# A four-layer gated model on one core: layer 2's folded-values product in three float32r passes, with its operands split on ScalarE, GpSimd and VectorE

## The chip, the core and the metric

One core of a Trainium2 chip runs the whole program in one launch. The metric is the device time of that launch in microseconds (us), lower is better; times of the kernel before are the median of three runs. All rows below come from one profiled execution. In them PE is TensorE (matmul), PEld its weight load, DVE VectorE, ACT ScalarE, POOL GpSimd, SP the engine that issues most DMAs.

## The reference, cut to what matters

Four layers of gated cross-attention and feed-forward on `x` (2 x 1024 rows of 256), with a context of 77 rows. The change lies in layer 2's attention and at the end of the feed-forward network (FFN) before it.

```python
x = x + tanh(g_xattn[0]) * attention0(layernorm(x), ctx)
x = x + tanh(g_ffn[0]) * fp4_ffn(layernorm(x))
x = x + tanh(g_xattn[1]) * attention1(layernorm(x), ctx)
x = x + tanh(g_ffn[1]) * (relu(layernorm(x) @ W1 + b1) @ W2 + b2)      # layer 1's FFN
# layer 2's attention: 16 heads of width 64, 77 keys
xn = layernorm2(layernorm(x)); q = xn @ w_q; k, v = split(ctx @ w_kv)
scores = einsum('bqhd,bkhd->bhqk', q / 8, k)
attn = softmax(scores, axis=-1)
out = einsum('bhqk,bkhd->bqhd', attn, v).reshape(B, SQ, 1024) @ w_out + b_out
x = x + tanh(g_xattn[2]) * out * tanh(gate)
x = x + tanh(g_ffn[2]) * (layernorm(x) @ w_int4 + bias + layernorm(x) @ a @ b)
x = x + ...layer 3's attention, then its mixture of experts
```

## The kernel before, in words

The 2048 rows of `x` lie in SBUF as 16 tiles of 128 rows. The program is a series of stages, one function for each engine and stage (`ffn1_tensor`, `ffn1_vector`, `att2_tensor`, ...). Inside a stage the engines run their own instruction lists, which are written out by hand, and meet on semaphores; at the end of a stage every engine drains and waits for the other four (`end_stage`, one semaphore `stage_done`).

Layer 1's FFN goes through four groups of four tiles. A group has eight units `m` of 128 hidden columns: PE multiplies up (L1987) and, two units later, down (L2003), both as three passes of rounded float32r parts (high x high, high x low, low x high); ACT does the relu (L2054) and rounds it to its high part (L2059); DVE makes the low part (L2107). In the last group the other work of DVE is the quantisation of layer 2's FFN kernel (units 3 to 5), the statistics of tiles 0 and 1 for layer 2 (`lead_vector`, unit 6), and after the last unit the normalised tile 0 (`ln_apply_one`, L318 and L320), which PE waits for before it turns it (L2036) and goes on with the last down product. POOL meanwhile makes the low part of the folded key matrix `A2` (L870) and at the end the two reciprocal roots (`lead_pool`, L305).

Layer 2's attention works with matrices folded in advance: `A2` is the query projection times the keys, so that a tile's scores for all 16 x 77 = 1232 pairs of head and key are one product (L1498, in three banks of 462, 462 and 308 columns, three float32r passes); `VO` is the values times the output projection, so that the output is the 1232 probabilities (ten blocks of 128 pairs) times `VO` (L1520, in plain float32, ten products of 128 x 128 by 256 columns for each tile). In step `t` of the stage:

- PE: scores of tile t in parts j = 0, 1, 2, and behind each part the transposes of tile t-1's probabilities for the same j (L1508; chunks of 3, 4 and 3 blocks, into banks 3, 4, 3); layer 2's small FFN product of tile t-3 (L1529, L1537); the transposes of normalised tile t+1 (L1564); the output product of tile t-1 (L1520) and its bias (L1522).
- ACT: for each j the copy of the transposed probabilities of tile t-1 to SBUF (L1585), then the exponentials of tile t, one instruction of 77 columns for each head (L1593), with the negative maximum as bias; between them the copy L1604 and the rounding of tile t+1 to its high part (L1479).
- DVE: the two additions to `x` (L1648, L1652), the maximum of each score part (L1629), statistics (L295 to L300), the normalised tile t+2 (L318, L320), the low part of tile t+1 (L1485), and for each j the softmax's sum over 77 keys (L1638), its reciprocal (L1639) and the multiplication of the probabilities (L1640).
- POOL: the reciprocal roots (L305).

The waits that matter below: PE turns probabilities j after `norm_done` of DVE; bank 3 (j = 2) is filled again only after the copy of chunk 0 (`pt_copied`); the output product of chunk j waits for `pt_copied` of that chunk; the scores of tile t+1 wait for `x_lo`, which DVE's L1485 of step t gives. Probabilities and their transposes have two buffers each.

The output product before:

```python
for j, (c0, c1) in enumerate(PT2_CHUNKS):
    pe.wait_ge(s["pt_copied"], 3 * t + j + 1)
    for k in range(c0, c1):
        pe.matmul(bank[6][:, 0:D], probT2[p][:, k, :], vo[:, bass.ds(v0 + k * D, D)],
                  start=k == 0, stop=False, skip_group_check=True)
```

Steps 0 to 3 and the last ones are written out; the steps between run in a hardware loop of two steps (`pipeline`).

## Time and profile before

| | us |
|---|---|
| median of three runs | 1105.09 (1104.5 to 1105.19) |
| the profiled execution, its own time | 1102.33 |
| its span | 1100.5 |
| PE busy / PEld busy | 1045.6 (95%) / 898.1 (82%) |
| DVE busy | 779.4 (71%) |
| ACT busy | 536.3 (49%) |
| POOL busy | 172.1 (16%) |
| share of PE in the chain that ended last | 87% |

The span is the time from the first to the last instruction of the profiled execution; 1.8 us of its own time lie around it, and it is 2.8 us below the median. "Busy" counts an engine's own instructions; a share over the whole program mixes stages. The chain is followed back from the last instruction, at each step to what released it. In the timelines a row is a start, a duration and the operation, and instructions of one engine may overlap: the next one starts some hundredths before the one ahead of it has ended. A bracket is idle time before the row and what ended it.

### The profile page before, as it was taken

The page shows a single profiled execution, that of the slowest core. Times are in us where ns is not written, and L with a number is a line of the kernel's source. Part 1 is how long each engine was busy: PE and PEld are TensorE (multiplying, and loading weights), DVE is VectorE, ACT ScalarE, POOL GpSimd, SP SyncE. Part 2 cuts the span into 40 slices and gives each one's busy share as a digit, 9 for nine tenths or more (in the row PEclk, how much of TensorE's full clock was granted, in tenths as well). Part 3 has the DMA queues.
Part 4 walks back from the last instruction along what each step waited for, and adds up shares of the span by engine and source line. Part 5 has one row for each costly group of instructions (what it writes and reads, how often), then busy time and mean ns, then how long its engine had stood idle before and what let it go on. Part 6 is the DMA issues. An engine that isn't in the chain of part 4 may idle for free.

```text
span 1100.5 us, 18719 instructions
## 1 busy us (share of the span) xinstructions
PE 1045.6 (95%) x6208; PEld 898.1 (82%) x6208; DVE 779.4 (71%) x1779; ACT 536.3 (49%) x1279; POOL 172.1 (16%) x255
## 2 busy tenths in 40 slices
PE   4987899999999999999999998999999999999998
PEld 4865567777999979888888887999778888888887
DVE  5786779998887855458888867878674575555544
ACT  4677655533555565545554544566543333334222
POOL 2232001101112142230111100132330010000000
PEclk9798899999999999999999999999999999999999
DMA  9401010002000000000000005000021121122120
GB/s 287 108 1 42 1 12 1 0 1 77 2 1 0 1 12 2 1 1 1 1 0 0 1 1 244 1 0 1 1 80 66 57 80 49 60 78 64 51 84 30
DMA packets 30377, 41.22 MB, mean 37 GB/s; under 512 B 13615, under 2 KB 19577, under 8 KB 29414
## 3 DMA queue, kind: packets, MB, share of 16 engines
q1 hardware_dynamic: 29437, 39.63, 11.5%
q10 hardware_dynamic: 873, 0.72, 0.3%
q8 instruction: 39, 0.64, 0.2%
q14 instruction: 28, 0.23, 0.1%
HBM read 37.80 MB, written 2.54 MB: 37 GB/s over the span
## 4 chain that ended last, share of the span: by engine, by line
PE 87%; DVE 4%; ACT 4%; issue 1%; SPq 1%; DMA 1%; POOL 0%; DVEq 0%; PEldq 0%; ACTq 0%; POOLq 0%; PEld 0%
PE psum L2197 17%; PE psum L2208 9%; PE psum L1734 7%; PE psum L380 6%; PE psum L1520 6%; PE psum L1297 6%; PE psum L1268 5%; PE psum L1498 5%; PE psum L1987 4%; PE psum L2003 4%; PE psum L1742 4%; PE psum L1279 3%; PE psum L1208 2%; PE psum L1508 2%; PE psum L1537 1%
## 5 line engine op out<-in xcount | busy, mean ns | idle before, releaser
L305 POOL TENSOR_TENSOR rstd<-ve,mhalf 128x1 f32<-128x1 f32 x114 | 75.7, 665 | 561.0 <-DVE ve L300 560.8
L391 ACT COPY work<-psum 128x256 f32<-128x256 f32 (+2 forms) x241 | 99.2, 438 | 117.9 <-PE psum L380 111.2
L380 PE MATMUL psum<-ident,work 128*128 128x128 f32 (+2 forms) x596 | 95.2, 282 | 9.8 <-ACT zone L605 3.5
L2279 ACT CAST h_hi<-work 128x512 fp32r<-128x512 f32 x68 | 42.2, 621 | 122.8 <-DVE work L2350 95.5
L2340 DVE TENSOR_TENSOR work<-psum,work 128x512 f32<-128x512 f32 x68 | 46.9, 689 | 75.0 <-ACT work L2271 74.9
L380 PEld LDWEIGHTS psum<-ident,work 128*128 128x128 f32 (+2 forms) x596 | 73.3, 147 | 22.2 <-DVE xT_lo L1228 3.8
L2197 PE MATMUL psum<-x_hi,ew_hi 128*128 128x512 f32 (+1 forms) x272 | 87.2, 401 | 0.2
L2197 PE MATMUL psum<-x_lo,ew_hi 128*128 128x512 f32 (+1 forms) x272 | 85.3, 395 | 0.0
L2197 PE MATMUL psum<-x_hi,ew_lo 128*128 128x512 f32 (+1 forms) x272 | 84.8, 393 | 0.0
L1734 PE MATMUL psum<-early,work 128*128 128x352 f32 x256 | 82.4, 477 | 1.4 <-ACT zone L605 0.9
L2208 PE MATMUL psum<-ew_hi,h_hi 128*128 128x256 f32 x272 | 76.9, 283 | 2.4 <-DVE h_lo L2357 2.4
L2208 PE MATMUL psum<-ew_hi,h_lo 128*128 128x256 f32 x272 | 77.3, 284 | 0.0
L2208 PE MATMUL psum<-ew_lo,h_hi 128*128 128x256 f32 x272 | 76.8, 282 | 0.0
L2357 DVE TENSOR_TENSOR h_lo<-work,h_hi 128x512 fp32r<-128x512 f32 x68 | 46.9, 690 | 42.1 <-ACT h_hi L2279 42.0
L1297 PEld LDWEIGHTS psum<-zone,work 128*128 128x128 f32 x640 | 74.0, 192 | 0.2
L1297 PE MATMUL psum<-zone,work 128*128 (+2 forms) x640 | 74.2, 272 | 0.0
L2271 ACT ACTIVATE work<-psum 128x512 f32<-128x512 f32 x68 | 40.6, 596 | 69.0 <-PE psum L2197 68.8
L1734 PEld LDWEIGHTS psum<-early,work 128*128 128x128 f32 x256 | 49.4, 198 | 27.9 <-issue 3.0
L1520 PE MATMUL psum<-zone,work 128*128 128x256 f32 (+1 forms) x320 | 71.7, 379 | 0.0
L1520 PEld LDWEIGHTS psum<-zone,work 128*128 128x128 f32 x320 | 59.5, 190 | 7.7
L1593 ACT ACTIVATE work<-psum,small 128x77 f32<-128x77 f32 x256 | 62.5, 379 | 5.9 <-DVE small L1629 5.9
L1585 ACT COPY work<-psum 128x384 f32<-128x384 f32 (+1 forms) x48 | 27.0, 564 | 73.0 <-PE psum L1508 73.0
(285 smaller groups left out, 2596.9 us busy)
## 6 DMA issues: line engine op xcount, KB each, us to landing
work<-expert_shares SPq DMA_DIRECT2D x64, 256.0 KB, 3.2
early<-in_experts_in SPq DMA_DIRECT2D x1, 6528.0 KB, 18.5
x<-in_x_in SPq DMA_DIRECT2D x4, 512.0 KB, 6.7
early<-in_W_in SPq DMA_DIRECT2D x2, 1024.0 KB, 7.1
out_x<-x SPq DMA_DIRECT2D x3, 512.0 KB, 4.3
early<-in_Wk SPq DMA_DIRECT2D x1, 1024.0 KB, 6.1
early<-in_Wq SPq DMA_DIRECT2D x1, 1024.0 KB, 8.7
zone<-in_Wv SPq DMA_DIRECT2D x1, 1024.0 KB, 13.1
```

The costliest lines, as they stand in the source:

```text
L305: pool.tensor_tensor(rstd[:, slot:slot + 1], ve[:, slot:slot + 1], mhalf[:, 0:1], ALU.pow).then_inc(s["rstd_ready"], 1)
L380: last = pe.transpose(dst[0:rows, at:at + n], src, ident[0:n, 0:n])
L391: act.copy(dst, src).then_inc(s["tr_copied"], 1)
L1268: last = pe.matmul(bank[j][:, (a - h0) * SK:(z - h0) * SK], q_[:, k, :], key[:, bass.ds(col + (a - h0) * SK, (z - a) * SK)], start=(k, a, ...
L1297: last = pe.matmul(dst, probT[:, k, :], Vb[l][:, bass.ds(v0 + (k * 3 + a - a0) * vw, (z - a + 1) * vw)], start=k == mine[0], stop=k == min ...
L1498: last = pe.matmul(bank[j][:, 0:n], x_[:, k, :], a[k][0][:, bass.ds(col + a[k][1], n)], start=i == 0 and k == 0, stop=i == 2 and k == KD - 1)
L1520: pe.matmul(bank[6][:, 0:D], probT2[p][:, k, :], vo[:, bass.ds(v0 + k * D, D)], start=k == 0, stop=False, skip_group_check=True)
L1593: last = act.activation(prob[p][:, h * SK:(h + 1) * SK], bank[j][:, (h - h0) * SK:(h - h0 + 1) * SK], ACT.Exp, bias=nmx[:, h:h + 1])
L1734: last = pe.matmul(bank[c][:, 0:HALF], xnT[1 - p][:, k, :], wguT[:, k, c * HALF:(c + 1) * HALF], start=k == 0, stop=k == 1)
L2197: last = pe.matmul(bank[2 * which + e % 2][:], weights(w, e, which, k), a[:, k, cols], start=n == 0, stop=n == len(passes) - 1)
L2208: last = pe.matmul(bank[6 + j // 2][:, (j % 2) * D:(j % 2 + 1) * D], h[slot(e)][:, j * P:(j + 1) * P], weights(w, e, 2), start=e == 0 and ...
L2340: dve.tensor_tensor(esg[e % 2] if e < NE else hf[0], bank[2 + e % 2][:], esg[e % 2], ALU.mult).then_inc(s["u_read"], 1)
```

## The change

1. The output product runs in three float32r passes for each of the ten blocks. ACT rounds the transposed probabilities to `pT_hi` (two buffers, `pt_hi_done`), DVE subtracts from the same bank to get `pT_lo` (one buffer), and `pt_copied` is now given by DVE (`low_probabilities`), one subtraction behind each maximum.
2. `VO` is rounded in ten pieces of 128 x 512: ACT makes `vo_hi` (four pieces at the end of layer 1's FFN, one in step 0, three in step 1, two in step 2), POOL makes `vo_lo` in steps 0 to 2 (five, three, two pieces), ahead of its roots of that step. PE waits for five low pieces before tile 0's output product and for ten before tile 2's.
3. The sum over the keys is taken from DVE: the exponentials give it as their accumulator output (`accum_out`).
4. In the last group of layer 1's FFN the statistics of tiles 0 and 1 move from unit 6 to unit 1, the two roots on POOL behind piece 11 of `A2`, and the normalised tiles 0 and 1 into units 6 and 7; step -1 of layer 2 no longer makes tile 1.
5. A semaphore that nothing waited for (`vb_ready`) goes, and `shift` moves by two columns.

```diff
@@ -205,6 +205,10 @@
+        VO_WORDS = B * KT * D
+        vo_raw = VO.rearrange("p a b -> p (a b)")
+        vo_hi = rounded("vo_hi", early_at, KD * B * HK, [P, VO_WORDS])
+        vo_lo = rounded("vo_lo", zone2_at, KD * B * HK + 8 * D, [P, VO_WORDS])
...
@@ -403,7 +403,9 @@ (buffers of the transposed probabilities)
-        probT2 = [probT, carve(work, [at[0] + 2 * D], (KT, P))]
+        pT_hi = [rounded(f"pT_hi{k}", work_at, word, [P, KT, P]) for k, word in
+                 enumerate((common + 2 * KT * P, at[0] + 2 * D))]
+        pT_lo = rounded("pT_lo", work_at, common + 3 * KT * P, [P, KT, P])
...
+        def vo_pieces(t):
+            return range(0) if not isinstance(t, int) else {0: range(5), 1: range(5, 8), 2: range(8, 10)}.get(t, range(0))
...
@@ att2_tensor, outputs
+                if isinstance(t, int) and t in (0, 2):
+                    pe.wait_ge(w_lo_done, LO_BEFORE["VO"] + VO_PIECES * (1 if t == 0 else 2))
...
-                        pe.matmul(bank[6][:, 0:D], probT2[p][:, k, :], vo[:, bass.ds(v0 + k * D, D)],
-                                  start=k == 0, stop=False, skip_group_check=True)
+                        for i, (pr, vo) in enumerate(three((pT_hi[p], pT_lo), (vo_hi, vo_lo))):
+                            pe.matmul(bank[6][:, 0:D], pr[:, k, :], vo[:, bass.ds(v0 + k * D, D)],
+                                      start=k == 0 and i == 0, stop=False, skip_group_check=True)
...
@@ att2_scalar
-                act.copy(probT2[p][:, c0:c1, :], bank[PT2_BANKS[j]][:, 0:(c1 - c0) * P].rearrange("p (a b) -> p a b", a=c1 - c0)
-                         ).then_inc(s["pt_copied"], 1)
+                act.copy(pT_hi[p][:, c0:c1, :], bank[PT2_BANKS[j]][:, 0:(c1 - c0) * P].rearrange("p (a b) -> p a b", a=c1 - c0)
+                         ).then_inc(s["pt_hi_done"], 1)
...
-                                          ACT.Exp, bias=nmx[:, h:h + 1])
+                                          ACT.Exp, bias=nmx[:, h:h + 1], accum_out=rs[:, h:h + 1])
...
             def step(t, p):
+                for n in vo_pieces(t)[VO_EARLY if isinstance(t, int) and t == 0 else 0:]:
+                    act.copy(vo_piece(vo_hi, n), vo_piece(vo_raw, n)).then_inc(w_hi_done, 1)
...
@@ att2_vector
-                link(dve, dve.tensor_reduce(rs[:, h0:h1], pr, AX_X, ALU.add))
...
+            def low_probabilities(t, p, j):
+
+                c0, c1 = PT2_CHUNKS[j]
+                src = bank[PT2_BANKS[j]][:, 0:(c1 - c0) * P].rearrange("p (a b) -> p a b", a=c1 - c0)
+                dve.wait_ge(s["pt_hi_done"], 3 * t + j + 1)
+                if j == 0:
+                    wait(dve, s["y_ready"], t)
+                dve.tensor_tensor(pT_lo[:, c0:c1, :], src, pT_hi[p][:, c0:c1, :].bitcast(F32),
+                                  ALU.subtract).then_inc(s["pt_copied"], 1)
...
                 if has(t):
                     maximum(t, 0)
+                if has(t - 1):
+                    low_probabilities(t - 1, 1 - p, 0)
...
-                if has(a) and not led(a + 1):
+                if has(a) and not led(a + 1) and not (isinstance(t, int) and t < 0):
...
                 if has(t):
                     maximum(t, 1)
+                if has(t - 1):
+                    low_probabilities(t - 1, 1 - p, 1)
+                if has(t):
                     normalise(t, p, 0)
                     maximum(t, 2)
+                if has(t - 1):
+                    low_probabilities(t - 1, 1 - p, 2)
...
@@ att2_pool
             for t in range(-1, T + 2):
+                for n in vo_pieces(t):
+                    pool.wait_ge(w_hi_done, HI_BEFORE["VO"] + n + 1)
+                    settle(pool, pool_waits_taken)
+                    pool.tensor_tensor(vo_piece(vo_lo, n), vo_piece(vo_raw, n), vo_piece(vo_hi, n).bitcast(F32),
+                                       ALU.subtract).then_inc(w_lo_done, 1)
...
@@ roots_groups
-            if then:
-                lead_pool(pool, then)
+                    if n == T - 5:
+                        lead_pool(pool, then)
...
@@ ffn1_scalar, behind turned_high(act, 0, ...)
+            for n in range(VO_EARLY):
+                act.copy(vo_piece(vo_hi, n), vo_piece(vo_raw, n)).then_inc(w_hi_done, 1)
...
@@ ffn1_vector
-                    if not front and m == 6:
+                    if not front and m == 1:
                         lead_vector(dve, a_s[2], True, False)
+                    if not front and m >= NM1 - 2:
+                        t = m - NM1 + 2
+                        ln_apply_one(dve, t, t, a_s[2], xn[t]).then_inc(a_s[2]["xn_ready"], 1)
...
-            ln_apply_one(dve, 0, 0, a_s[2], xn[0]).then_inc(a_s[2]["xn_ready"], 1)
             turned_low(dve, 0, 0, bank[4][:, 0:D])
```

Where the lists move, on VectorE in step 2 of layer 2's attention (`small` holds maxima and sums, `work` the probabilities and normalised tiles, `st` the statistics), before and then now:

```order
L1629 TENSOR_REDUCE small<-psum 128x6
L1638 TENSOR_REDUCE small<-work 128x6
L1639 RECIPROCAL small<-small 128x6
L1640 TENSOR_TENSOR work<-work,small 128x462
L1629 TENSOR_REDUCE small<-psum 128x4
L295 BN_STATS st<-x 128x6
```

```order
L1646 TENSOR_REDUCE small<-psum 128x6
L1666 TENSOR_TENSOR pT_lo<-psum,pT_hi_63 128x512
L1655 RECIPROCAL small<-small 128x6
L1656 TENSOR_TENSOR work<-work,small 128x462
L1646 TENSOR_REDUCE small<-psum 128x4
L1666 TENSOR_TENSOR pT_lo<-psum,pT_hi_63 128x384
L299 BN_STATS st<-x 128x6
```

The sum L1638 has gone and a subtraction stands behind each maximum, ahead of the work that follows it.

On ScalarE from the end of layer 1's FFN into steps 0 and 1, before and then now:

```order
L2078 COPY gwT<-psum 128x32
L1479 CAST xT_hi_65<-psum 128x256
L1593 ACTIVATE work<-psum,small 128x77 x12
L1479 CAST xT_hi_66<-psum 128x256
L1593 ACTIVATE work<-psum,small 128x77 x4
L1585 COPY work<-psum 128x384
```

```order
L2116 COPY gwT<-psum 128x32
L1492 CAST xT_hi_70<-psum 128x256
L2119 CAST vo_hi<-zone 128x512 x4
L1614 CAST vo_hi<-zone 128x512
L1608 ACTIVATE work,small<-psum,small 128x77 x12
L1492 CAST xT_hi_71<-psum 128x256
L1608 ACTIVATE work,small<-psum,small 128x77 x4
L1614 CAST vo_hi<-zone 128x512 x3
L1600 CAST pT_hi_63<-psum 128x384
```

Each exponential now has a second output in `small`, and eight roundings of `VO` stand before tile 0's probabilities are taken.

On VectorE at the end of layer 1's FFN (L2107, now L2147, is the low part of a unit, L2098, now L2138, the addition to `x`), before and then now:

```order
L2107 TENSOR_TENSOR r_lo_75<-work,r_hi_73 128x512
L295 BN_STATS st<-x 128x6
L297 BN_AGGR mv<-st 128x2
L300 TENSOR_SCALAR ve<-mv 128x1
L295 BN_STATS st<-x 128x6
L297 BN_AGGR mv<-st 128x2
L300 TENSOR_SCALAR ve<-mv 128x1
L2107 TENSOR_TENSOR r_lo_76<-work,r_hi_74 128x512
L318 TENSOR_SCALAR small<-mv,rstd 128x1
L320 TENSOR_SCALAR work<-x,rstd,small 128x256
L1485 TENSOR_TENSOR xT_lo_67<-psum,xT_hi_65 128x256
```

```order
L2147 TENSOR_TENSOR r_lo_80<-work,r_hi_78 128x512
L322 TENSOR_SCALAR small<-mv,rstd 128x1
L324 TENSOR_SCALAR work<-x,rstd,small 128x256
L2147 TENSOR_TENSOR r_lo_81<-work,r_hi_79 128x512
L322 TENSOR_SCALAR small<-mv,rstd 128x1
L324 TENSOR_SCALAR work<-x,rstd,small 128x256
L1498 TENSOR_TENSOR xT_lo_72<-psum,xT_hi_70 128x256
L2138 SCALAR_TENSOR_TENSOR x<-psum,tg,x 128x256 x4
```

Tile 0 is normalised a unit earlier, and tile 1 before the additions instead of after the stage's end.

## Rows read from the trace of the kernel before

**Rows 1.** Busy time by engine in the stage of layer 2's attention

```profile
core 0: us, PE busy (x) PEld busy (x) DVE busy (x) ACT busy (x) POOL busy (x), PEclk, DMA share, GB/s
494.70:668.00 173.30, 169.77 (x949) 148.93 (x950) 142.59 (x386) 87.10 (x339) 18.50 (x34) 1.00 0.00 1
```

**Rows 2.** The chain in order of time: start, us, what

```profile
506.94 4.32 PE psum L1520 x20
...
526.38 4.32 PE psum L1520 x20
...
639.93 4.32 PE psum L1520 x20
...
829.82 1.43 PE psum L2208 x12
```

**Rows 3.** Timeline of DVE, one step of layer 2's attention: start, us, operation, idle before

```profile
561.92 0.48 DVE L1648 SCALAR_TENSOR_TENSOR x<-psum,tg,x 128x256 f32 x1 [0.51 <-PE psum L1522]
...
563.07 0.64 DVE L1629 TENSOR_REDUCE small<-psum 128x6 f32<-128x462 f32 x1 [0.28 <-PE psum L1498]
...
565.08 0.63 DVE L1629 TENSOR_REDUCE small<-psum 128x6 f32<-128x462 f32 x1
...
567.59 0.42 DVE L295 BATCH_NORM_STATS2 st<-x 128x6 f32 x1
...
568.78 0.62 DVE L1638 TENSOR_REDUCE small<-work 128x6 f32<-128x462 f32 x1
569.43 0.19 DVE L1639 RECIPROCAL small<-small 128x6 f32<-128x6 f32 x1
...
570.54 0.46 DVE L1638 TENSOR_REDUCE small<-work 128x4 f32<-128x308 f32 x1
571.04 0.18 DVE L1639 RECIPROCAL small<-small 128x4 f32<-128x4 f32 x1
...
572.25 0.48 DVE L1648 SCALAR_TENSOR_TENSOR x<-psum,tg,x 128x256 f32 x1 [0.52 <-PE psum L1522]
```

**Rows 4.** Groups of instructions by form, the DVE subtraction from PSUM, 256 and 512 columns

```profile
L1485 DVE TENSOR_TENSOR xT_lo<-psum,xT_hi 128x256 fp32r<-128x256 f32 x15 | 6.2, 414 | 0.0
...
L2340 DVE TENSOR_TENSOR work<-psum,work 128x512 f32<-128x512 f32 x68 | 46.9, 689 | 75.0 <-ACT work L2271 74.9
```

**Rows 5.** Timeline of ACT in layer 0's FFN, an accumulator read; one exponential alone

```profile
108.13 0.51 ACT L1782 ACTIVATE work<-x,small 128x256 f32<-128x256 f32 x1
108.54 0.19 ACT L1782 ACTIVATION_READ_ACCUMULATOR work<-x,small 128x1 f32 x1
108.64 0.35 ACT L391 COPY work<-psum 128x256 f32<-128x256 f32 x1
...
578.29 0.35 ACT L1593 ACTIVATE work<-psum,small 128x77 f32<-128x77 f32 x1
```

**Rows 6.** Timeline of ACT, the same step

```profile
564.31 1.42 ACT L1593 ACTIVATE work<-psum,small 128x77 f32<-128x77 f32 x6
565.56 0.64 ACT L1585 COPY work<-psum 128x512 f32<-128x512 f32 x1
566.03 1.47 ACT L1593 ACTIVATE work<-psum,small 128x77 f32<-128x77 f32 x6
567.28 0.59 ACT L1585 COPY work<-psum 128x384 f32<-128x384 f32 x1
```

**Rows 7.** Groups by form: roundings of 512 columns on ACT, splits on POOL

```profile
L2059 ACT CAST r_hi<-work 128x512 fp32r<-128x512 f32 x32 | 19.9, 621 | 21.4 <-PE psum L2003 21.3
...
L870 POOL TENSOR_TENSOR w_lo<-early,w_hi 128x256 fp32r<-128x256 f32 x16 | 11.6, 747 | 8.7 <-ACT w_hi L864 8.6
```

**Rows 8.** Timelines of PE and DVE around the end of layer 1's FFN

```profile
491.77 0.44 PE L2036 MATMUL psum<-ident,work 128*128 128x128 f32 x2 [1.55 <-DVE work L320]
...
494.75 0.69 PE L1498 MATMUL psum<-a_hi,xT_hi 128*128 128x462 f32 x2 [1.14 <-SPq L236]
...
494.87 0.22 DVE L318 TENSOR_SCALAR small<-mv,rstd 128x1 f32<-128x1 f32 x1 [0.22 <-SPq L236]
```

More of the change, by code:

```diff
@@ L245, in flamingo @@
         w_lo_done = sem("w_lo_done")
-        HI_BEFORE = {"W12": 0, "A2": 16, "experts": 16 + T}
+        VO_PIECES = 5
+        HI_BEFORE = {"W12": 0, "A2": 16, "VO": 16 + T, "experts": 16 + T + B * VO_PIECES}
         LO_BEFORE = HI_BEFORE
@@ L272, in flamingo @@
         FRONT = ("stat_ready", "rstd_ready", "xn_ready", "tr_filled", "tr_copied")
-        set_s = stage_sems("setup", "filled", "read", "prep", "wq_scaled", "kb_hi_done", "scalar_chain", "vp_zero",
-                           "vb_ready")
+        set_s = stage_sems("setup", "filled", "read", "prep", "wq_scaled", "kb_hi_done", "scalar_chain", "vp_zero")
         q_s = stage_sems("fp4w", "m_ready", "r_ready", "ready", "misc", "amax", "gw", "tables")
@@ L316, in ln_apply_one @@
             wait(dve, s["rstd_ready"], t + 1)
-            shift = small[:, 26 + slot:27 + slot]
+            shift = small[:, 28 + slot:29 + slot]
             link(dve, dve.tensor_scalar(shift, mv[:, slot, 0:1], rstd[:, slot:slot + 1], 1.0 / D, ALU.mult,
@@ L877, in flamingo @@
         W12_LEAD = 6
+        VO_EARLY = 4
         SETUP_BANKS = (2, 5)
@@ L1472, in flamingo, with vo_piece @@
         PT2_BANKS = (3, 4, 3)
+        def vo_pieces(t):
+            return range(0) if not isinstance(t, int) else {0: range(5), 1: range(5, 8), 2: range(8, 10)}.get(t, range(0))
+        def vo_piece(a, n):
+            return a[:, n * KT * D // VO_PIECES:(n + 1) * KT * D // VO_PIECES]
         x2_bank = bank[5][:, 0:D]
@@ L1576, in att2_scalar @@
             s, f = a_s[2], f_s[2]
-            nmx = small[:, 32:48]
+            nmx, rs = small[:, 32:48], small[:, 48:64]
             def take_probabilities(t, p, j):
@@ L1682, in step @@
                     normalise(t, p, 2)
-            pipeline(dve, -1, step, [(chain_n, 2 * (6 + 4 + 1))], T + 3, AHEAD)
+            pipeline(dve, -1, step, [(chain_n, 2 * (3 + 4 + 1))], T + 3, AHEAD)
             end_stage(dve, "dve")
```

8 lines of the change are left out of this document (3 added, 5 removed).

## The prediction

> **What bounds the kernel now.** I read the busy time by stage, then the chain, then one step's timelines of DVE and ACT. In layer 2's attention PE is busy 169.8 of 173.3 us [rows 1], and the chain runs from one output product to the next on PE: from 526.38 to 639.93 us there are eleven steps, so a step takes 10.32 us, 4.32 of them the output product [rows 2]. PE sets the pace, but DVE is close behind: between two additions (561.92 and 572.25) it idles only 0.52 and 0.28 us, both times for PE [rows 3]. So a shorter product on PE can gain at most until DVE, or a path through DVE, ends last. ACT has room in its sum, and that sum is not what counts: its instructions stand inside a path.
>
> **The product on PE.** Before: ten float32 products, 20 records, 4.32 us. Now: 30 float32r products of the same size. Layer 3's experts show 12 of these, with their weight loads, in 1.43 us [rows 2], 0.119 each; 30 take 3.58. PE's step becomes 10.32 - 0.74 = 9.58 us. In the loop of steps PE also has two register operations in front of every three products; I cost them at nothing, since their cover is the 0.119 us of each product, and take 0.2 us a step as the upper bound.
>
> **DVE's own step.** Idle time makes the next start about 0.08 us later than it would be without, so the work of a step is 10.33 - 0.52 - 0.28 - 0.16 = 9.37 us. Off go the three sums over the keys: 568.78 to 569.43 is 0.65 us, the one like it again 0.65, 570.54 to 571.04 is 0.50, in all 1.80. On come three subtractions from PSUM of 384, 512 and 384 columns: 0.414 us for 256 and 0.689 for 512 [rows 4], so 0.55 for 384; the next instruction starts 0.07 before the end, so 0.48, 0.61 and 0.48, in all 1.57. DVE's step is then 9.14 us, below 9.58.
>
> **What the accumulator output costs ACT.** The trace before has no such exponential, but ACT in layer 0's FFN shows that an accumulator output is a second instruction, a read of 0.19 us, which starts 0.10 us before its ACTIVATE ends and is followed 0.10 us after its own start [rows 5]. Six exponentials run from 566.03 to 567.28, 0.21 us apart [rows 6], though one alone takes 0.35 [rows 5]. If the read only adds its own 0.10, an exponential costs a = 0.09 to 0.10 more; if it also takes the overlap between neighbours away, a pair costs 0.35 - 0.10 + 0.19 - 0.10 = 0.34, so a = 0.13. Without any overlap of the read a = 0.19, which is my upper bound. I take a = 0.11, between the first two, because both overlaps stand in the rows of the read. With 16 exponentials ACT has 1.8 us more in a step.
>
> The Trainium skill's page "ScalarE: Activation LUTs", section "What ACT_TABLE_LOAD costs", gives an ACTIVATE with a pointer bias about 280 ns + 0.833 ns a column, and 93 ns of overlap back to back. By it 77 columns cost 0.34 us alone, as the trace has it, but 0.25 in a row of them where the trace has 0.21; with the read of 0.19 the pair would take 0.345, so a = 0.137 and a loop of 10.1 us in place of 9.90. The trace disagrees with its 0.25 for the row of exponentials.
>
> **The new loop.** DVE's subtraction waits for ACT's rounding, which stands behind exponentials, which wait for DVE's maximum. One turn of it:
> - DVE from the last subtraction (0.48) over statistics, low part of x, two multiplications and the second norm to the next addition: 567.59 to 572.25 is 4.66, less two sums (0.65 + 0.50), less 0.52 idle and 0.08, is 2.91 [rows 3].
> - from the addition to the second maximum, 561.92 to 565.08, 3.16 less 0.28 and 0.08, is 2.80 [rows 3], and the first subtraction in between, 0.48.
> - the second maximum whole, 0.63, and 0.05 to hand over.
> - ACT's six exponentials 1.25 + 6a, then the last rounding whole, 0.59, and 0.05 [rows 6].
>
> Sum 9.24 + 6a. The other branch goes from the first maximum over exponentials and the middle rounding (1.25 + 6a, then 565.56 to 566.03, 0.47) to the second set of exponentials; it is longer once a is over 0.13, and then the loop is 8.48 + 12a. With a = 0.11 the loop takes 9.90 us, more than PE's 9.58: PE will wait about 0.3 us in each step, in front of the last three blocks of the output product, and the step falls from 10.32 to 9.90, not to 9.58.
>
> **The sum in layer 2's attention.** Steps 3 to 15, twelve intervals: 12 x 0.42 = 5.0 us off. Ramp: in step 0 DVE loses two sums while ACT gains 12 reads (1.3 us) ahead of tile 1's rounding, and step 1 has three roundings of VO of 0.62 us [rows 7] in front of tile 0's probabilities; together I take +0.2 us (bounds -0.5 and +1.5). End: the last output products run with no exponentials behind them, so their 0.74 comes nearly whole, and the last step with exponentials is short of one wait: 1.2 off. Net 6.0 us off.
>
> **The end of layer 1's FFN.** PE's 1.55 us of waiting for the normalised tile goes [rows 8], since that tile is now made in unit 6. Next is DVE: low part, four additions, then the stage's end; they follow PE's last product, so nearly all of it is kept. ACT's four roundings of VO (0.62 each, 2.2 in a row) begin when tile 0's high part is done and end about with those additions; their cover is those additions, and without it they would cost some 0.5 us. The statistics of unit 1 go into idle time of DVE, whose low parts there wait for ACT in every unit; without it they would delay one low part by about 1 us, and PE uses that two units later. Tile 1's normalisation (0.6 us from 494.87 [rows 8]) leaves the start of the next stage; its gain is in the ramp. Taken: 1.5 us off, bounds 0.8 and 2.0.
>
> **POOL.** Ten subtractions of 512 columns: 0.75 us for 256 [rows 7], so about 1.3 each, an estimate. Five stand before the first root of step 0 and tile 0's product: from the stage's start some 1.5 + 6.5 = 8 us, and that product begins 12 us after it (506.94 after 494.75 [rows 2, 8]). The root of tile 3 comes late but is wanted a step later. Nothing on the path; if POOL were twice as slow, about 2 us.
>
> **The number.** 6.0 + 1.5 = 7.5 us off. The sum is made on the profiled execution, 1102.33 us, 2.8 below the median of the runs; taken off the median it gives 1097.6 us. A measurement here tells about 0.2%, 2.2 us, from no change.
>
> **Rivals.**
> - Forecast, DVE and ACT's loop at 9.8 to 10.0 us (a = 0.09 to 0.12): 1096 to 1099.5, chance 0.50.
> - PE stays the bound at 9.58, if a is at most 0.05, or the subtractions are cheaper than I think: 13 x 0.74 + 2 at the ends + 1.5 is 13 us off, 1092. For it: exponentials overlap more than the rows of other instructions; against: each read is an instruction of its own. Chance 0.13.
> - The read breaks the overlap of its neighbours, a = 0.13 to 0.15: loop 8.48 + 12a = 10.04 to 10.28. The gain of a step is 0.28 to 0.04 and the ramp grows by 1; total 5 to 1 off, 1100 to 1104, its middle 1102. The 0.13 is worked out above, the 0.15 adds the rounding of its rows. 
> - The other side: the read costs its whole 0.19. Then ACT's path is 8.48 + 2.28 = 10.76 us, 0.44 longer than before, PE waits some 1.2 us in each step: 13 x 0.44 + 2.3 in the ramp - 1.5 is 6.5 slower, 1111.6. It is slower by over 2.2 us once a passes about 0.165. For it: the accumulator must hold the whole row before it is read; against: the read overlaps by 0.10 on either side [rows 5]. Chance 0.13.
> - The change doesn't do what it says, the three passes taking no less than the 4.32 us, because of register operations: loop and PE then at about 10.3, only the FFN's end gains, 1103.5. Against: twelve products in 1.43. Chance 0.04.
>
> **How the numbers follow.** Faster by over 0.2%: 0.50 + 0.13 and two thirds of the third case, 0.77. Same: the rest of that case and the last, 0.10. Slower 0.13. The range leaves out the slower case and the outer edge of the PE-bound one: 1091.5 to 1105.
>
> **What would show it.** The page after should have 256 accumulator reads; the distance between two exponentials' starts in ACT's timeline gives a. Right: the output product at 0.119 us a record with a wait on DVE's subtraction (L1666) in front of its last blocks, steps of 9.9 us, ACT idle 2 to 3 us a step, no wait at the end of layer 1's FFN. Wrong: steps of 9.58 with no wait on PE (the loop is shorter), or of 10.3 and more (a over 0.14).

## The result, and the profile after

| | before | after |
|---|---|---|
| median, us (runs) | 1104.80 (4) | 1097.29 (4; 1093.17 to 1098.14) |
| ratio after / before, 95% interval | | 0.9932 (0.9915 to 0.9949) |
| the profiled execution, its span | 1102.33, 1100.5 | 1093.17, 1091.4 |

The change takes 7.5 us off the median, as forecast; by the interval of the ratio it is 5.6 to 9.4. The profiled execution of after is the fastest of its four, 9.1 us of span shorter than that of before, so I split the span first. Busy time by stretch, of after: the front of the program, layer 2's attention, the rest.

```profile
core 0: us, PE busy (x) PEld busy (x) DVE busy (x) ACT busy (x) POOL busy (x), PEclk, DMA share, GB/s
0.00:94.70 94.70, 69.69 (x352) 55.07 (x353) 65.85 (x180) 58.43 (x157) 27.17 (x46) 0.96 0.40 115
490.74:658.03 167.29, 161.63 (x1106) 147.87 (x1106) 141.20 (x383) 115.00 (x601) 32.32 (x44) 0.99 0.00 1
658.03:1091.40 433.37, 422.63 (x2660) 373.72 (x2660) 271.37 (x612) 175.81 (x319) 54.30 (x51) 1.00 0.18 60
```

And of before:

```profile
0.00:94.70 94.70, 72.21 (x350) 57.74 (x350) 65.65 (x179) 58.29 (x156) 26.77 (x43) 0.87 0.40 115
494.75:667.44 172.69, 169.22 (x946) 148.42 (x946) 142.16 (x385) 86.75 (x339) 18.50 (x34) 1.00 0.00 1
667.44:1100.50 433.06, 422.56 (x2660) 373.86 (x2660) 271.16 (x612) 175.78 (x319) 54.78 (x51) 1.00 0.19 60
```

Layer 2's attention is 5.40 us shorter (172.69 to 167.29). It begins 4.01 us earlier: 1.55 us is the wait at the end of layer 1's FFN [rows 8], which is gone. Of the other 2.46, 2.3 lie in the first 137 us, in code that the change doesn't touch: the two traces are that far apart at 137 us and still at 468 us. The first 94.7 us ran at a mean granted clock of 0.96 against 0.87, so this part belongs to the execution and not to the change. Timeline of PE, after:

```profile
487.79 0.38 PE L2074 MATMUL psum<-ident,work 128*128 128x128 f32 x2
...
490.74 0.69 PE L1511 MATMUL psum<-a_hi,xT_hi 128*128 128x462 f32 x2 [1.14 <-SPq L240]
```

**The size of a.** Timeline of ACT in after, the row that stood 0.21 us apart before [rows 6]:

```profile
561.24 0.35 ACT L1608 ACTIVATE work<-psum,small 128x77 f32<-128x77 f32 x1
...
561.54 0.35 ACT L1608 ACTIVATE work<-psum,small 128x77 f32<-128x77 f32 x1
...
561.84 0.36 ACT L1608 ACTIVATE work<-psum,small 128x77 f32<-128x77 f32 x1
```

The exponentials are 0.30 apart, so a = 0.09, though a read by itself is listed with 0.229. Groups by form, after (busy us, mean ns, idle before them and its releaser): all 256 of both, and the two forms of DVE's subtraction:

```profile
L1608 ACT ACTIVATE work<-psum,small 128x77 f32<-128x77 f32 x256 | 80.4, 349 | 3.8 <-DVE small L1646 3.3
L1608 ACT ACTIVATION_READ_ACCUMULATOR work<-psum,small 128x1 f32 x256 | 58.6, 229 | 0.0
...
L1666 DVE TENSOR_TENSOR pT_lo<-psum,pT_hi 128x384 fp32r<-128x384 f32 x32 | 17.7, 554 | 8.3 <-ACT pT_hi L1600 8.1
...
L1666 DVE TENSOR_TENSOR pT_lo<-psum,pT_hi 128x512 fp32r<-128x512 f32 x16 | 11.0, 688 | 1.4 <-ACT pT_hi L1600 1.1
```

**One step.** Timeline of PE, after, in the program's loop:

```profile
557.36 0.28 PE L1537 MATMUL psum<-brow,ones 96*128 96x256 bf16 x1
557.54 0.69 PE L1511 MATMUL psum<-a_hi,xT_hi 128*128 x2
...
563.44 0.36 PE L1535 MATMUL psum<-vo_hi,pT_hi 128*128 x1
...
567.05 0.28 PE L1537 MATMUL psum<-brow,ones 96*128 96x256 bf16 x1
567.37 0.69 PE L1511 MATMUL psum<-a_hi,xT_hi 128*128 x2
...
616.04 0.28 PE L1537 MATMUL psum<-brow,ones 96*128 96x256 bf16 x1
616.08 0.66 PE L1511 MATMUL psum<-a_hi,xT_hi 128*128 128x462 f32 x2
```

The product takes 563.44 to 567.05, 3.61 us for 30 records. In the loop 0.18 and 0.32 us pass from the start of a step's last product (the bias) to the next scores; behind the loop, at 616.04, only 0.04. Timeline of DVE, the same step and the first row of the next:

```profile
558.87 0.48 DVE L1674 SCALAR_TENSOR_TENSOR x<-psum,tg,x 128x256 f32 x1
...
562.14 0.63 DVE L1646 TENSOR_REDUCE small<-psum 128x6 f32<-128x462 f32 x1
...
565.16 0.56 DVE L1666 TENSOR_TENSOR pT_lo<-psum,pT_hi 128x384 fp32r<-128x384 f32 x1 [0.51 <-ACT pT_hi L1600]
...
566.49 0.41 DVE L1498 TENSOR_TENSOR xT_lo<-psum,xT_hi 128x256 fp32r<-128x256 f32 x1
...
568.76 0.48 DVE L1674 SCALAR_TENSOR_TENSOR x<-psum,tg,x 128x256 f32 x1 [0.16 <-issue]
```

And of ACT in the same step, the first exponential behind the second maximum and the last rounding:

```profile
562.81 0.32 ACT L1608 ACTIVATE work<-psum,small 128x77 f32<-128x77 f32 x1
...
564.62 0.50 ACT L1600 CAST pT_hi<-psum 128x384 fp32r<-128x384 f32 x1
```

DVE no longer waits for PE, as it did in [rows 3], but for ACT's last rounding (0.51 us), and ACT's exponentials start 0.04 us after DVE's second maximum has ended.

**The ramp.** The timelines of DVE, POOL and PE in steps 0 and 1 of after, and PE's granted clock (PEclk) around PE's wait:

```profile
495.18 1.57 DVE L1656 TENSOR_TENSOR work<-work,small 128x462 f32<-128x462 f32 x1
...
498.45 1.15 DVE L1656 TENSOR_TENSOR work<-work,small 128x462 f32<-128x462 f32 x1
```

```profile
492.46 6.64 POOL L1726 TENSOR_TENSOR vo_lo<-zone,vo_hi 128x512 fp32r<-128x512 f32 x5
```

Two of these five, the one that was running when DVE's multiplication began and the one behind it:

```profile
495.00 1.26 POOL L1726 TENSOR_TENSOR vo_lo<-zone,vo_hi 128x512 fp32r<-128x512 f32 x1
...
496.22 1.66 POOL L1726 TENSOR_TENSOR vo_lo<-zone,vo_hi 128x512 fp32r<-128x512 f32 x1
```

```profile
498.38 1.14 PE L1511 MATMUL psum<-a_hi,xT_hi 128*128 128x462 f32 x2 [2.06 <-DVE xT_lo L1498]
499.31 0.97 PE L1511 MATMUL psum<-a_lo,xT_hi 128*128 128x462 f32 x2
```

```profile
495.08:498.38 3.30, 1.24 (x7) 0.40 (x5) 3.08 (x8) 3.15 (x21) 3.30 (x3) 0.96 0.00 0
498.38:501.68 3.30, 3.30 (x10) 2.88 (x11) 2.34 (x5) 1.67 (x5) 3.30 (x4) 0.53 0.00 0
```

Two things here are new. DVE's multiplication of 462 columns takes 1.57 and 1.15 us while POOL works on VO, and 0.64 elsewhere. And PE's wait is 2.06 us instead of 1.65. In the 3.3 us behind it the granted clock is 0.53, so nearly all of them ran at the lower level, 1.2 GHz: 0.97 us for two score products that take 0.58 at full clock.

### The profile page after: what moved, and what is told of

Same layout as the page of the kernel before. It is cut to its first block, busy times and chain, and to the rows that moved or that the text cites. A ratio compares the mean times of both kernels' runs of the same rounds, so it can differ in the third digit from the quotient of the medians.

```text
span 1091.4 us, 19407 instructions
## 1 busy us (share of the span) xinstructions
PE 1031.6 (95%) x6368; PEld 892.3 (82%) x6368; DVE 779.8 (71%) x1779; ACT 566.7 (52%) x1545; POOL 185.3 (17%) x265
## 4 chain that ended last, share of the span: by engine, by line
PE 50%; DVE 3%; ACT 1%; DMA 0%; issue 0%; PEldq 0%; DVEq 0%; PEld 0%; ACTq 0%; SPq 0%
PE psum L2239 17%; PE psum L2250 8%; PE psum L1535 5%; PE psum L1511 5%; PE psum L1303 3%; PE psum L1274 3%; PE psum L384 2%; PE psum L1521 1%; PE psum L1552 1%; PE psum L1285 1%; PE psum L1214 1%; ACT work L1608 1%; PE psum L2194 0%; PE psum L1544 0%; DMA work<-expert_shares 0%
## 5 line engine op out<-in xcount | busy, mean ns | idle before, releaser
L1608 ACT ACTIVATE work<-psum,small 128x77 f32<-128x77 f32 x256 | 80.4, 349 | 3.8 <-DVE small L1646 3.3
L1772 PE MATMUL psum<-early,work 128*128 128x352 f32 x256 | 80.0, 466 | 1.4 <-ACT zone L611 0.9
L1303 PEld LDWEIGHTS psum<-zone,work 128*128 128x128 f32 x640 | 74.0, 192 | 0.2
L2239 PEld LDWEIGHTS psum<-x_hi,ew_lo 128*128 128x128 f32 x272 | 51.3, 189 | 12.1
L2239 PEld LDWEIGHTS psum<-x_lo,ew_hi 128*128 128x128 f32 x272 | 51.3, 189 | 11.5
L1408 DVE TENSOR_REDUCE small<-psum 128x6 f32<-128x462 f32 (+1 forms) x96 | 55.7, 580 | 6.7 <-PE psum L1274 6.7
```

The costliest lines, as they stand in the source:

```text
L1303: last = pe.matmul(dst, probT[:, k, :], Vb[l][:, bass.ds(v0 + (k * 3 + a - a0) * vw, (z - a + 1) * vw)], start=k == mine[0], stop=k == min ...
L1408: link(dve, dve.tensor_reduce(mx[:, h0:h1], sc, AX_X, ALU.max))
L1608: last = act.activation(prob[p][:, h * SK:(h + 1) * SK], bank[j][:, (h - h0) * SK:(h - h0 + 1) * SK], ACT.Exp, bias=nmx[:, h:h + 1], accum ...
L1772: last = pe.matmul(bank[c][:, 0:HALF], xnT[1 - p][:, k, :], wguT[:, k, c * HALF:(c + 1) * HALF], start=k == 0, stop=k == 1)
L2239: last = pe.matmul(bank[2 * which + e % 2][:], weights(w, e, which, k), a[:, k, cols], start=n == 0, stop=n == len(passes) - 1)
```

## The experiments

All steps are measured from the first score product of one to that of the next, in the timeline of PE of each profiled execution. "Ramp" is steps 0 to 2 together, "loop" the mean of the eight steps of the program's loop (4 to 11), "behind" the mean of steps 12 and 13, whose code is written out; "stage" is from the first scores to layer 3's first key product. The ratio is to runs of before on the same chip.

| kernel | median | ratio (95%) | stage | ramp | loop | behind |
|---|---|---|---|---|---|---|
| before | 1104.80 | | 172.69 | 25.50 | 10.32 | 10.32 |
| after | 1097.29 | 0.9932 (0.9915, 0.9949) | 167.29 | 27.76 | 9.80 | 9.58 |
| after, again | 1095.33 | 0.9933 (0.9915, 0.9951) | 167.26 | 27.75 | 9.80 | 9.58 |
| FFN's tail alone | 1101.87 | 0.9987 (0.9975, 1.0) | 172.35 | 25.15 | 10.32 | 10.32 |
| sums back on DVE | 1114.01 | 1.0092 (1.0077, 1.0108) | 183.33 | 28.74 | 10.92 | 10.68 |
| no sums | 1092.22 | 0.9892 (0.9865, 0.9919) | 162.33 | 25.19 | 9.56 | 9.58 |
| two passes | 1094.84 | 0.9913 (0.989, 0.9937) | 166.18 | 27.73 | 9.79 | 9.59 |
| statistics first | 1095.88 | 0.9925 (0.991, 0.9939) | 167.04 | 26.22 | 9.94 | 9.71 |
| PE written out | 1095.84 | 0.9926 (0.9906, 0.9945) | 166.00 | 26.55 | 9.78 | 9.61 |
| all written out | 1094.34 | 0.9915 (0.9898, 0.9932) | 165.00 | 26.51 | 9.65 | 9.59 |
| thin subtractions | 1090.96 | 0.9892 (0.9876, 0.9908) | 164.50 | 24.95 | 9.80 | 9.59 |
| 16 fillers | 1096.23 | 0.9937 (0.9917, 0.9958) | 166.10 | 26.54 | 9.80 | 9.59 |
| spread | 1090.81 | 0.9885 (0.9866, 0.9903) | 163.61 | 25.21 | 9.65 | 9.60 |
| before written out | 1104.23 | 1.001 (0.9996, 1.0024) | 172.69 | 25.49 | 10.32 | 10.32 |

The times of one kernel spread over some 5 us. The traces show where: in the kernels whose code is the same up to there, the stage starts anywhere from 490.74 (after) to 495.52 us (two passes), and behind the stage the executions differ by another 2.7 us. So the stage and its steps tell apart what the medians can't.

**1. The end of layer 1's FFN alone,** on the kernel before.

```diff
-                if has(a) and not led(a + 1):
+                if has(a) and not led(a + 1) and not (isinstance(t, int) and t < 0):
...
-            if then:
-                lead_pool(pool, then)
+                    if n == T - 5:
+                        lead_pool(pool, then)
...
-                    if not front and m == 6:
+                    if not front and m == 1:
                         lead_vector(dve, a_s[2], True, False)
+                    if not front and m >= NM1 - 2:
+                        t = m - NM1 + 2
+                        ln_apply_one(dve, t, t, a_s[2], xn[t]).then_inc(a_s[2]["xn_ready"], 1)
...
-            ln_apply_one(dve, 0, 0, a_s[2], xn[0]).then_inc(a_s[2]["xn_ready"], 1)
```

> The kernel before with only the change at the end of layer 1's FFN (statistics in unit 1, tiles 0 and 1 normalised in the last two units, roots there). If the tail is worth the 1.55 us that PE waited for the normalised tile, the time is 1.5 us below before (bounds 0.8 and 2.0), the wait of 1.55 us in front of the transposes of tile 0 is gone, and the next stage's first scores start that much earlier. Rival: the wait only moves, to the additions or the low part behind it: no change. The rest of the gain of the change, some 6 us, then belongs to layer 2's attention.

Measured: 0.9987, which is 1.4 us, with an interval from no gain to 2.8; the step 0 that lost tile 1's normalisation is 0.34 us shorter (6.89 against 7.23). The medians agree with 1.5 for the tail but don't prove it; the traces do: the wait of 1.55 us is gone in this run as in after.

**2. Where the sums over the keys stand.** On the change, once the sums go back to DVE, once they are left out on both engines.

```diff
-                                          ACT.Exp, bias=nmx[:, h:h + 1], accum_out=rs[:, h:h + 1])
+                                          ACT.Exp, bias=nmx[:, h:h + 1])
...
+                link(dve, dve.tensor_reduce(rs[:, h0:h1], pr, AX_X, ALU.add))
```

> The change with the sums over the keys put back on DVE and no accumulator output on ACT. If DVE with its three subtractions is near the bound, its step becomes 9.14 + 1.80 = 10.9 us, longer than the 10.32 of the kernel before: 13 steps of 1.1 us more than the 9.8 of the change, so about 1111 to 1113 us, slower than before. PE then waits over 1 us a step for DVE. Rival: DVE has slack enough that the sums cost nothing and the accumulator reads were not needed: 1097 us, steps of 9.6 to 9.8.

Measured: loop steps of 10.92 us against 10.9 expected (10.68 behind the loop), and 1114.01 us, 1 above the range expected. With the sums on DVE the three-pass product makes the kernel slower than before; moving them to ACT is what lets it pay.

> Leaves out the sums over the keys altogether: no accumulator output on ACT and no sums on DVE, the reciprocals are taken of what stands in their place. So a = 0. By the prediction's loop, 9.24 + 6a, the loop becomes 0.54 us shorter than with a = 0.09, PE's own 9.58 binds, with 0.14 for its register operations in the program's loop: steps of 9.7 there in place of 9.8, and PE never waits for DVE's subtraction: about 1.0 us less than the change in the eight steps, and up to 1 us in the ramp. Rival: the reads lie beside other work and are not on the loop: steps of 9.8 with the same waits, no change.

Measured: every step from 3 on takes 9.54 to 9.59 us, in the loop too, and the gap ahead of the scores is 0.04 in all of them. Six exponentials take 1.26 us where they took 1.81, which gives a = 0.09 a second time. So the reads are on the path. PE's own step is 9.56, and no register operations of 0.14 us stand in it while its operands are ready early (here DVE's xT_lo ended 0.64 to 0.76 us ahead of the scores in the loop): that part of the expectation was wrong.

**3. The third pass left out,** so that PE's own work is far below the rest.

```diff
-                        for i, (pr, vo) in enumerate(three((pT_hi[p], pT_lo), (vo_hi, vo_lo))):
+                        for i, (pr, vo) in enumerate(three((pT_hi[p], pT_lo), (vo_hi, vo_lo))[:2]):
```

> Leaves out the third pass of the product (high part of VO by low part of the probabilities); DVE still makes that low part and PE still waits for it. PE's own step falls by 10 x 0.119 to 8.4 us, so what is left is the loop through DVE and ACT alone. The loop as the prediction worked it out, with the measured a = 0.09, is 9.24 + 0.54 = 9.78 us: then the steps stay at 9.8, in the loop of the program and outside it, and the time is that of the change within 1 us. DVE's work alone would give 9.14 + 0.15: steps of 9.2 to 9.3, 1091 to 1092. Steps below 9.1 would say that both are wrong.

Measured: 9.79 in the loop, 9.59 behind it. PE has 1.2 us less work in a step, and the steps are no shorter for it. The waits of this run, 525 to 615 us (engine, line, waited for: us in total, times, longest):

```profile
PE psum L1535 <- DVE pT_lo L1666: 5.6, 9, 0.8
DVE pT_lo L1666 <- ACT pT_hi L1600: 5.0, 9, 0.6
...
PE psum L1511 <- DVE xT_lo L1498: 1.9, 7, 0.3
```

PE waits for DVE in every step, for the last low part of the probabilities and then for the input's low part, and DVE waits for ACT. This is the loop of the prediction, measured by itself: 9.8 us inside the program's loop, 9.6 in written-out code.

The same run shows what the gap ahead of the scores is. DVE's low part and PE's scores, first inside the loop, then behind it:

```profile
561.65 0.41 DVE L1498 TENSOR_TENSOR xT_lo<-psum,xT_hi 128x256 fp32r<-128x256 f32 x1
...
562.36 0.47 PE L1511 MATMUL psum<-a_hi,xT_hi 128*128 x1 [0.23 <-DVE xT_lo L1498]
```

```profile
620.28 0.41 DVE L1498 TENSOR_TENSOR xT_lo<-psum,xT_hi 128x256 fp32r<-128x256 f32 x1
...
620.75 0.48 PE L1511 MATMUL psum<-a_hi,xT_hi 128*128 128x462 f32 x1
```

Behind the loop the scores start 0.06 us after the low part has ended, inside it 0.30 (0.29 to 0.35 over the eight steps). So where PE's operand comes late, PE loses another 0.24 us a step in its own loop, which it doesn't where the operand is early (the run without sums, where the gap is 0.04). In after this is most of the gap: DVE's low part had ended 0.29 to 0.46 us before the scores.

**4. The loops of the program written out.**

```diff
-            pipeline(pe, 0, step, [(Count(), 0)], T + 2, AHEAD)
+            pipeline(pe, 0, step, (), T + 2, AHEAD)
```

> The change with PE's four trips of two steps written out, so that PE's columns and waits are constants and no register operation is left there; DVE and ACT keep their loops. In the change the steps of the loop take 9.80 us on average and those outside it 9.58; in the loop 0.12 to 0.32 us pass between the last product of a step and the next scores, outside 0.04. Theory 1: these are PE's register operations, about 0.14 us a step, and in every second step 0.27 more is a wait for DVE's last subtraction: the gap falls to 0.04, and 8 x 0.14 = 1.1 us go, unless they come back as longer waits for DVE. Theory 2, of the prediction: the DVE-ACT loop alone sets 9.8 us: no change.

Measured: the gaps fall to 0.04, but every second step now takes 10.0 us and the mean is 9.78. The time came back as a longer wait for the last subtraction. So PE's share of theory 1 falls: what PE loses in its loop isn't on the path.

> As the one before, with the loops of DVE and ACT written out too. Theory 1: what makes a step in the loop 9.80 us in place of 9.58 are register operations on the three engines, so all steps become 9.58: 8 x 0.22 = 1.8 us less than the change, about 1095.5. Theory 2, that the arithmetic of DVE and ACT sets 9.8: no change. Rival 3: four times the code of a trip on each engine has to be loaded, and costs more than that: slower.

Measured: 9.65 in the loop. Seven of the steps 3 to 11 take 9.54 to 9.62 us, as behind the loop; the other two take 9.77 and 9.90, because DVE stands still in them for 0.35 us more between two rows of its statistics, which are 0.56 apart everywhere else:

```profile
586.40 0.42 DVE L299 BATCH_NORM_STATS2 st<-x 128x6 f32<-128x256 f32 x1
587.31 0.18 DVE L301 BATCH_NORM_AGGREGATE mv<-st 128x2 f32<-128x6 f32 x1 [0.50 <-DVE st L299]
```

What holds it there stays open; the version of experiment 8 stands still in the same two steps. So the loops of ACT and DVE were worth the whole 0.2 us a step, and 0.06 of it came back as these pauses. In after it can be seen on DVE: in every second step of the loop L324 starts 0.39 us after L322 (0.24 behind the loop), and in the others the addition starts late with nothing to wait for:

```profile
571.44 0.21 DVE L322 TENSOR_SCALAR small<-mv,rstd 128x1 f32<-128x1 f32 x1
571.83 0.42 DVE L324 TENSOR_SCALAR work<-x,rstd,small 128x256 f32 x1 [0.17 <-DVE small L322]
```

PE's part of theory 1 is wrong, that of the other two stands. The kernel before with its three loops written out is the control:

> The kernel before with the loops of PE, ACT and DVE in layer 2's attention written out, as in the fastest version. If written-out loops help only because the path through DVE and ACT sets the step of the changed kernel, they are worth nothing here, where PE sets it: steps of 10.32 as before, no change within 0.2%, and what the fastest version gains over the change rests on the change. Rival: register operations hold back the kernel before as well, in its three sums and its maxima on DVE: 1 to 2 us less.

Measured: steps of 10.32, ratio 1.001. Where PE sets the step, this buys nothing.

**5. Statistics ahead of the third subtraction,** an attempt to fill DVE's wait.

```diff
-                if has(t - 1):
-                    low_probabilities(t - 1, 1 - p, 2)
                 if has(a + 1) and not led(a + 1):
                     ln_stats(dve, a + 1, (p + AHEAD) % 2, s, twice=True)
...
+                if has(t - 1):
+                    low_probabilities(t - 1, 1 - p, 2)
```

> The change with one move on DVE: the layer norm statistics of tile t+3 (about 0.85 us until the next instruction) stand ahead of the third subtraction, which waits for ACT's rounding, in place of behind it. If the loop through DVE and ACT sets the step (9.8 us in the trace, PE's own work 9.58), the statistics fill the wait of 0.5 to 0.6 us, the loop loses them, and the step falls to about 9.6: 12 times 0.2 is 2.4 us less than the change, about 1095. Rival 1: PE itself sets the 9.8, then nothing moves. Rival 2: the subtraction comes later by what the statistics exceed the wait (0.3 us), and PE waits that much in front of its last blocks each step: up to 3 us more than the change.

Measured: 9.94 in the loop, 0.14 more. DVE's wait did not go, it moved to the first subtraction; timeline of DVE in this run:

```profile
621.29 0.56 DVE L1666 TENSOR_TENSOR pT_lo<-psum,pT_hi 128x384 fp32r<-128x384 f32 x1 [0.47 <-ACT pT_hi L1600]
...
626.52 0.55 DVE L1666 TENSOR_TENSOR pT_lo<-psum,pT_hi 128x384 fp32r<-128x384 f32 x1
```

Rival 2 had the direction, with half its 0.3 us a step. The ramp gained 1.5 against after, but 1.2 of that is the clock (below), so the move itself bought nothing.

**6. POOL's subtractions made thin.**

```diff
-                        for i, (pr, vo) in enumerate(three((pT_hi[p], pT_lo), (vo_hi, vo_lo))):
+                        for i, (pr, vo) in enumerate(three((pT_hi[p], pT_lo), (vo_hi, vo_hi))):
...
-                    pool.tensor_tensor(vo_piece(vo_lo, n), vo_piece(vo_raw, n), vo_piece(vo_hi, n).bitcast(F32),
+                    pool.tensor_tensor(vo_piece(vo_lo, n)[:, 0:32], vo_piece(vo_raw, n)[:, 0:32], vo_piece(vo_hi, n)[:, 0:32].bitcast(F32),
```

> Leaves out the low part of the folded values: POOL's ten subtractions are of 32 columns in place of 512, and the second pass of the product takes the high part again, so PE has the same 30 products. If POOL's long subtractions stretch DVE's instructions with two inputs from SBUF (1.57 us in place of 0.64 in step 0), and so delay the low part of tile 1's input, PE's wait of 2.06 us there falls to about 1.1 to 1.5, the granted clock stays at 1.0 behind it, and steps 0 to 2 together are 2 to 3 us shorter than in the change: 1094 to 1095. Rival: step 0 is set by ACT's twelve exponentials with their reads, ahead of the rounding of tile 1: the wait stays at about 2 us, the clock falls all the same, and the time with it stays within 0.5 us.

Measured: ramp 24.95, which is 2.8 us less than after. DVE's multiplication is back at 0.64 and PE's wait at 1.22; timelines of this run:

```profile
496.39 0.64 DVE L1656 TENSOR_TENSOR work<-work,small 128x462 f32<-128x462 f32 x1
```

```profile
498.74 0.69 PE L1511 MATMUL psum<-a_hi,xT_hi 128*128 128x462 f32 x2 [1.22 <-DVE xT_lo L1498]
```

Against the runs whose clock stayed up (ramp 26.5) it is 1.6 us: that is the price of POOL in the ramp.

**7. More fillers behind tile 0's scores, and the change once more.**

```diff
-                    keep_busy(pe, 8)
+                    keep_busy(pe, 16)
```

> The change with 16 instead of 8 filler products behind tile 0's scores. In the change PE waits 2.06 us there for tile 1's low part, and the granted clock reads 0.50 (1.2 GHz) for the next 3.3 us, in which scores that take 2.78 us at full clock take 4.3. Theory: the wait is what brought the clock down; eight more fillers of 0.215 us take 1.7 us of the wait, the clock stays at 2.4 GHz, and the stage is about 1.5 us shorter: 1095.8. Rival 1: PE in step 1 then only waits for DVE and ACT, which POOL and the exponentials hold up: under 0.5 us. Rival 2: the fillers end behind tile 1's low part and cost time.

Measured: the wait falls to 0.35, the clock stays at 1.00, step 1 takes 9.14 instead of 10.36 and the stage is 1.2 us shorter. The median shows nothing of it (0.9937): 1.2 us is less than it can resolve, and the clock may not fall in every execution:

> The change itself, once more, on the chip of these runs, so that the spread of its steps and its time can be set beside theirs: 1093 to 1098.5 us. If the fall of the granted clock behind PE's 2.06 us of waiting follows from the wait, it shows again and step 1 takes 10.3 us; if it comes by chance, step 1 may take 9.14.

Measured: it shows again, step 1 takes 10.35. But with PE written out, where PE waited 2.07 us in the same place, the 3.3 us behind it ran at full clock:

```profile
501.32:504.62 3.30, 3.30 (x19) 2.94 (x20) 3.19 (x8) 3.04 (x12) 3.30 (x4) 1.00 0.00 0
```

Of the seven profiled executions with that wait (2.05 to 2.07), the clock fell in three (after, again, two passes) and stayed in four. It costs 1.2 us where it falls. What decides between them stays open. So the fillers were shown to take the wait away, not that they alone kept the clock up in that execution.

**8. A version that is faster than before and the change.** Written-out loops, 12 fillers, and POOL's work moved: piece 0 to the FFN's last unit, 1 and 2 in step 0, 3 and 4 in step 1, the other five one to a step.

```diff
-            return range(0) if not isinstance(t, int) else {0: range(5), 1: range(5, 8), 2: range(8, 10)}.get(t, range(0))
+            return {0: (1, 2), 1: (3, 4), **{n - 3: (n,) for n in range(5, 10)}}.get(t, ())
...
+                if t == 1:
+                    pool.wait_ge(s["x_lo"], 2)
+                if 2 <= t <= 6:
+                    pool.wait_ge(s["max_done"], 3 * t + 1)
```

> The written-out loops of the run before, and POOL's ten subtractions of the folded values placed elsewhere: one in the last unit of layer 1's FFN, two in step 0, two in step 1 behind tile 1's low part, and one in each of steps 2 to 6, behind DVE's first maximum, where DVE reads PSUM; ACT's roundings go with them; 12 fillers in place of 8 in step 0. From the run with thin subtractions (first three steps 24.95 us in place of 26.5) and the one with written-out loops (stage 165.0 us): stage 163.4 us, 1.6 less, so 1092.5 to 1093. Rival 1: a subtraction in the middle of a step stretches DVE there and each costs 0.3 to 0.9 us: gain lost, 1094 to 1097. Rival 2: the subtraction in the FFN's last unit ends behind the last addition and delays the stage by 0.3 us.

Measured: 1090.81, 1.7 below the range expected, against 1095.33 of the change on the same chip, and the intervals of the two ratios don't meet; stage 163.61 (163.4 expected) against 167.26, of which 2.5 us in the ramp (1.2 of them the clock) and 1.2 in the loop. The ramp is within 0.3 us of that with thin subtractions. Rival 1 came true once, in step 1, where a multiplication of 308 columns took 1.22 us; rival 2 did not, for the stage starts 1.4 us after the start of the FFN's last product, as in after. Timeline of POOL in this run, one piece in its new place:

```profile
522.48 1.29 POOL L1491 TENSOR_TENSOR vo_lo<-zone,vo_hi 128x512 fp32r<-128x512 f32 x1 [2.54 <-DVE small L1653]
```

## Why the prediction was right, point by point

- **The total.** 7.5 us off was forecast and 7.5 measured. In the traces the stage gives 5.40, where 6.0 stood, and the FFN's end 1.55; the sum, 6.95, is within the spread of the runs. The terms of the stage did not all hold, as follows.
- **The product on PE.** Forecast 3.58, measured 3.61; PE's own step 9.58 as forecast. Register operations cost that step nothing, the lower bound held; where PE's operand came late they may be what its loop shows (0.24 us in experiment 3), but that isn't on the path.
- **DVE's step.** The subtractions last 0.554 and 0.688 (0.55 and 0.69 were taken). With the sums put back DVE is never idle for more than 0.2 us, and the step is 10.92 in the program's loop, where 9.14 + 1.80 = 10.94.
- **a.** 0.11 taken, 0.09 measured, the lower bound: the read takes away no overlap of its neighbours. The rivals from 0.13 up fall, and with them the estimate of 0.137 and of a loop of 10.1 us, worked out from the figures of the Trainium skill's page "ScalarE: Activation LUTs", section "What ACT_TABLE_LOAD costs"; this trace disagrees with it.
- **The new loop.** The path is shown: with PE's load cut the steps stay at 9.79, and with a = 0 the loop is no longer the bound and PE's 9.56 shows. The sum, 9.24 + 6a = 9.78 with a = 0.09, meets the measured 9.80 by luck, as the turn taken apart in the rows of after shows:

| part of the turn, us | forecast | loop, 558.87 | loop, 568.76 | written out, 617.48 |
|---|---|---|---|---|
| addition to second maximum | 3.28 | 3.27 | 3.40 | 3.21 |
| maximum to its exponentials | 0.68 | 0.67 | 0.66 | 0.67 |
| six exponentials | 1.79 | 1.81 | 1.81 | 1.82 |
| last rounding to its subtraction | 0.64 | 0.54 | 0.54 | 0.53 |
| subtraction to next addition | 3.39 | 3.60 | 3.36 | 3.36 |
| turn | 9.78 | 9.89 | 9.77 | 9.59 |

The bare turn is 9.59. The forecast's terms are 0.2 too long, half of it in the last rounding: I took the whole 0.59 of the copy before, and the rounding lasts 0.50. The program's loop adds 0.2 to 0.3 for which the sum had no term. Where PE pays was only half right: in front of the last three blocks in every second step (0.27 us at 556 us), the rest in front of the next scores. ACT idles 2.7 us a step waiting for PE, as forecast.
- **Where it holds.** The step that failed is "12 x 0.42". I used one figure, 9.90, for all twelve steps. In written-out code the turn is 0.2 us shorter than in the program's loop and no longer than PE's step, so steps 3 and 12 to 14 lost 0.71 and 2.17 us, 1.2 more than four times 0.42. The eight of the loop lost 4.18 (82.57 to 78.39), 0.8 more, since they take 9.80 and not 9.90. In all 7.06 instead of 5.0.
- **The ramp.** +0.2 was forecast (upper bound +1.5), +2.26 measured. "Nothing on the path" for POOL was the mistake: I asked whether its results came in time, which they did, and not what it slows down. That is 1.6 us without the clock, and 1.2 more where the clock falls. Without both the ramp is 0.55 us shorter than before (24.95 against 25.50), and that much is paid back.
- **The end.** 1.2 was forecast and 0.60 measured behind step 14. The two last products are 0.57 and 0.70 us shorter, so that term held. What was missing is a wait: ahead of tile 15's last transposes PE waited 0.28 us for ACT's copy before and now waits 0.87 us for DVE's subtraction, which empties their bank. PE's timeline, before and after:

```profile
655.72 0.52 PE L1508 MATMUL psum<-ident,work 128*128 128x128 f32 x3 [0.28 <-ACT work L1585]
```

```profile
647.09 0.52 PE L1521 MATMUL psum<-ident,work 128*128 128x128 f32 x3 [0.87 <-DVE pT_lo L1666]
```

- **The FFN's end.** 1.5 was forecast, 1.55 of waiting is gone, and alone it measured 1.4.

So the right number is in part luck: it rests on two errors of some 2 us that cancel. Steps 3 to 14 gained 2.1 more than forecast, the ramp lost 2.1 more.

## What to carry to other kernels

When an engine's load is cut, write down the loop through the other engines as a sum of rows and check it twice: by a run in which the first engine has far less to do, and by one in which the suspected term is zero. An engine that "has room" is priced by its place in such a loop, and work put on GpSimd also by what VectorE runs at that moment. A sum that meets the measured step isn't thereby right: set it beside the new trace term by term. And what holds inside a loop of the program (9.8 us here) need not hold in written-out code (9.6).

## What the runs showed of the hardware

- An accumulator output costs ScalarE 0.09 us a time in a row of exponentials of 77 columns (0.30 apart instead of 0.21; six take 1.81 us with it and 1.26 without), though the read is listed with 0.23.
- A subtraction of 512 columns on GpSimd with both inputs in SBUF takes 1.3 us and holds up VectorE's multiplication with two SBUF inputs: 1.57 and 1.15 us instead of 0.64 (462 columns), and once 1.37 instead of 0.48 (308 columns). VectorE's instructions that read PSUM beside it kept their times (0.63 and 0.47 for the maxima). By the Trainium skill's page "SBUF — State Buffer", section "SBUF: two separate sides", such a pair shares ports under an exclusive lock, held by whichever started first for its whole instruction. The trace agrees: the subtraction had begun at 495.00, the multiplication at 495.18, and 1.57 is 0.64 and 0.93 of the subtraction's 1.26 us; the next subtraction took 1.66.
- A normalisation with one SBUF tensor input was stretched as well, from 0.41 to 0.79 and 1.06 us.
- Behind a wait of 2.05 to 2.07 us TensorE's granted clock fell to its lower level (1.2 GHz; 0.53 on average over 3.3 us) in three of seven executions, and stayed at 2.4 GHz in four; behind waits of 0.35 to 1.65 us it stayed there in all seven other executions.
- A loop of the program costs little where an engine's operands are early, and shows where they are late: TensorE's scores started 0.29 to 0.35 us after the instruction that they waited for inside the loop, and 0.06 in written-out code. On the path through VectorE and ScalarE the loop cost 0.2 us in a step of 9.8.
